# A third buffer for the key rows, and weights and x loaded ahead of the last four transfers of zeros, in a four-layer graph network

## The reference, cut to what matters

```
gathered = edge_weight[:, None] * x[edge_col]
neigh = segment_sum(gathered, edge_row, 3125)
out = x @ w_self + neigh @ w_neigh + bias        # weight = [w_self; w_neigh], 512 x 256
x = layernorm(x + out)
```

## Time and profile before

| | |
|---|---|
| Median of 3 runs | 3868.58 us (3865.46, 3868.58, 15440.14) |
| Profiled execution | 3860.42 us, span 3858.6 us |
| Instructions | 61183 |
| Busy in the span | PE 81%, PEld 47%, DVE 59%, ACT 37%, POOL 44% |
| DMA | 621.76 MB, mean 161 GB/s |
| Mean granted clock of TensorE | 0.891 of full speed |

### The profile page before, as it was taken

The page is one execution under the profiler, slowest core; times in us unless marked ns, Lnnn a source line. Parts: engine busy times, 40 slices in busy tenths (PEclk is TensorE's granted clock), DMA queues, the critical chain, the costliest instruction groups (busy, mean ns, idle before and its releaser), DMA issues. The chain is left out here.

```text
span 3858.6 us, 61183 instructions
## 1 busy us (share of the span) xinstructions
PE 3120.0 (81%) x16127; PEld 1811.6 (47%) x16128; DVE 2281.6 (59%) x5544; ACT 1443.9 (37%) x3080; POOL 1694.2 (44%) x1703
## 2 busy tenths in 40 slices
PE   4547999988997787777779957769864799998996
PEld 2114444666775343376634435644333444544543
DVE  7556333567898987655799965689867401202104
ACT  0000222478897565431056634036644402302202
POOL 3777772055002777616777752767772000000000
PEclk6678999999999898878989978779976899999998
DMA  9997889388654345366711105944452231231221
GB/s 400 404 365 258 311 295 302 100 248 247 174 148 115 101 138 153 105 241 194 211 25 27 27 18 189 309 139 138 128 178 84 84 97 44 82 97 53 92 89 34
DMA packets 381401, 621.76 MB, mean 161 GB/s; under 512 B 129149, under 2 KB 259926, under 8 KB 374098
## 3 DMA queue, kind: packets, MB, share of 16 engines
q1 hardware_dynamic: 229881, 353.10, 28.8%
q0 software_dynamic: 68112, 130.86, 11.9%
q10 hardware_dynamic: 83213, 135.59, 9.5%
HBM read 453.68 MB, written 169.22 MB: 161 GB/s over the span
## 5 line engine op out<-in xcount | busy, mean ns | idle before, releaser
L1464 ACT ACTIVATE onehot<-iota,drel 128x128 f32<-128x128 f32 x1248 | 381.5, 388 | 715.8 <-PE ps L1167 374.4
L1167 PE MATMUL ps<-shared_sb,onehot 128*128 128x264 f32 (+1 forms) x1600 | 558.8, 448 | 105.4 <-DVE accum L2252 100.5
L1227 PE MATMUL ps<-score_sb,shared_sb 128*128 128x512 f16 (+1 forms) x3150 | 624.9, 359 | 12.0 <-DVE shared_sb L2284 12.0
L2252 DVE TENSOR_TENSOR accum<-accum,ps 128x264 f32 (+1 forms) x1248 | 526.0, 421 | 12.1 <-issue 4.7
L740 POOL DMA_INDIRECT t_w<-early_sb x391 | 411.8, 1053 | 163.8 <-issue 89.6
L1227 PEld LDWEIGHTS ps<-score_sb,shared_sb 128*128 128x128 bf16 x3150 | 297.6, 98 | 335.0 <-issue 11.7
L1167 PEld LDWEIGHTS ps<-shared_sb,onehot 128*128 128x128 f32 x1600 | 266.2, 202 | 397.7 <-issue 233.4
L757 POOL TENSOR_SCALAR onehot<-iota,carry_d 98x512 bf16<-98x512 f32 x28 | 43.5, 1561 | 902.2 <-PE ps L1244 801.4
L776 POOL DMA_INDIRECT score_sb<-table,src_x x192 | 200.2, 1043 | 325.9 <-issue 300.8
L776 POOL DMA_INDIRECT shared_sb<-table,src_x x312 | 299.2, 959 | 100.4 <-issue 89.5
L2238 DVE TENSOR_TENSOR shared_sb<-shared_sb,ps 128x256 f32<-128x256 f32 x512 | 211.5, 413 | 67.9 <-DMA shared_sb<-table,src_x 50.4
(11 more groups left out here) (425 smaller groups left out, 5484.0 us busy)
## 6 DMA issues: line engine op xcount, KB each, us to landing
t_w<-onehot ACTq DMA_DIRECT2D x13, 6400.0 KB
score_sb<-t_adj SPq DMA_DIRECT2D x90, 640.0 KB, 3.9
accum<-t_hot SPq DMA_DIRECT2D x208, 256.0 KB
t_hot<-shared_sb SPq DMA_DIRECT2D x104, 256.0 KB
resid_sb<-t_w SPq DMA_DIRECT2D x13, 1664.0 KB
resid_sb<-t_w SPq DMA_DIRECT2D x13, 1536.0 KB
score_sb<-t_w SPq DMA_DIRECT2D x12, 1664.0 KB
shared_sb<-t_adj SPq DMA_DIRECT2D x30, 640.0 KB, 9.2
```

The lines of the kernel that those rows point to most:

```text
L1167: pe.matmul(ps[:, RING[(HU * h + u) % len(RING)], 0:w], onehot[:, h % 2 * HU + u, :], around[g][place(g, i, h)][:, u, 0:w], start=True, st ...
L1227: mm = pe.matmul(ps[:, 2 * (i % 3) + f, 0:w], h_gin[:, t, m, f * P:(f + 1) * P], ring["gin"][:, at % HOLD, c, 0:w], start=(t == 0 and m == ...
L1464: last = act.activation(onehot[:, h % 2 * HU + u, :], iota[:, 0:P], ACT.Abs, bias=drel[:, bass.ds(step + u, 1)], scale=-1.0)
L2252: dve.tensor_tensor(to, to, bank.unsqueeze(1), ALU.add).then_inc(step_acc, 1)
```

## The change

There are three buffers of key rows in place of two (`KEYS` = 3); the third takes the unused space of `key_gap`. Load i waits for the comparisons of load i-3. Its third semaphore is `adj_in[4]`, whose later use counts on from there. The third load waits besides for `values`, since the space is used for the weights' parts before. ACT's code for comparisons and the waits on `key_used` and `same_act` go. The block of ACT's other transfers becomes a function, `late_loads`, that is called in the loop of zeros at n = 9: nine transfers of zeros have then been issued and eight have landed; four are issued after it. None of the transfers changes its size or form.

```
+KEYS = 3
+LATE = 9
-        wide_key = [... for buf in (shared_sb[:, 2176:...], resid_sb[:, 5120:...])]
-        key_gap = flat_a[:, 4224:4224 + 2 * L0H * P].rearrange("p (u e) -> p u e", u=2)
+        wide_key = [... for buf in (shared_sb[:, 2176:...], resid_sb[:, 5120:...],
+                                    flat_a[:, 4224:4224 + 2 * L0H * P])]
...
             def two_quads(i):
-                if i >= 2:
-                    sp.wait_ge(*count("same_dve", 2 * i - 2))
-                    sp.wait_ge(*count("key_used", 2 * i - 2))
-                sp.dma_start(wide_key[i % 2]..., on_each(t_key, i * 2 * L0H, 2 * L0H)).then_inc(key_in[i % 2], 16)
+                if i == KEYS - 1:
+                    sp.wait_ge(*count("values", 1))
+                if i >= KEYS:
+                    sp.wait_ge(*count("same_dve", 2 * i - 2 * KEYS + 2))
+                sp.dma_start(wide_key[i % KEYS]..., on_each(t_key, i * 2 * L0H, 2 * L0H)).then_inc(key_in[i % KEYS], 16)
...
+            def late_loads():
+                act.wait_ge(*count("attr_split", 1))
+                act.wait_ge(*count("adj_ev", 1))
+                act.dma_start(t_attr...)      # attr_out
+                act.dma_start(rows[:, :, :], a["rows"])      # ld_rows
+                act.dma_start(vecs[:, :, :], a["vecs"])      # ld_vecs
+                act.dma_start(weights[:, :, 0:D], a["L0_gnn_weight"]...)      # ld_w0
+                act.dma_start(cols[:, :, :], a["x_cols"]...)      # ld_x
+                act.dma_start(hrows[:, :, 0:D], a["x_pad"]...)      # ld_xh
             for n in range(PIECES + 2):
                 if n >= 2:
                     act.wait_ge(attr_in[n % 2], 16 * (n // 2))
                     act.sem_inc(done("w_zero"), 1)
+                if n == LATE:
+                    late_loads()
                 if n < PIECES:
                     act.dma_start(parts_w[(n - 1) % PIECES], no_sums).then_inc(attr_in[n % 2], 16)
-            (the same two waits and six transfers, here, behind the loop)
...
             def compare(k):      # DVE
-                dve.wait_ge(key_in[k // 2 % 2], 16 * (k // 4) + 16)
+                dve.wait_ge(key_in[k // 2 % KEYS], 16 * (k // 2 // KEYS) + 16)
```

More of the change, by code:

```diff
@@ L47 @@
 QUADS = ET // L0H
-FIRST = QUADS
+KEYS = 3
 BATCHES = [2, 2, 4] + [8] * 11 + [2]
@@ L238, in build @@
         lo_rows_i = flat_k[0:SQ, 5472:5984].rearrange("p (b e) -> p b e", b=SB).bitcast(I32)
-        wide_key = [buf.rearrange("p (h e) -> p h e", h=2) for buf in (shared_sb[:, 2176:2176 + 2 * L0H * P], resid_sb[:, 5120:5120 + 2 * L0H * P])]
-        key_gap = flat_a[:, 4224:4224 + 2 * L0H * P].rearrange("p (u e) -> p u e", u=2)
+        wide_key = [buf.rearrange("p (h e) -> p h e", h=2) for buf in (shared_sb[:, 2176:2176 + 2 * L0H * P], resid_sb[:, 5120:5120 + 2 * L0H * P],
+                                                                      flat_a[:, 4224:4224 + 2 * L0H * P])]
         ring = {"gcn": shared_sb[:, 0:HOLD * GRP * CW // 2].bitcast(F16).rearrange("p (r c w) -> p r c w", r=HOLD, c=GRP),
@@ L298, in build @@
         key_in = [sem(f"key_in{h}") for h in range(2)]
-        in_four, so_far = attr_in + key_in, [16 * len(range(h, PIECES, 2)) for h in range(2)] + [16 * len(range(n, QUADS // 2, 2)) for n in range(2)]
+        in_four, so_far = attr_in + key_in, [16 * len(range(h, PIECES, 2)) for h in range(2)] + [16 * len(range(n, QUADS // 2, KEYS)) for n in range(2)]
         adj_in = [sem(f"adj_in{r}") for r in range(HOLD)]
         adj_kept = adj_in[0:len(STAGED)]
-        kept_before = [16 * PAIRS] * len(STAGED) + [0] * (HOLD - len(STAGED))
+        key_in = key_in + [adj_in[len(STAGED)]]
+        kept_before = [16 * PAIRS] * len(STAGED) + [16 * len(range(2, QUADS // 2, KEYS))] + [0] * (HOLD - len(STAGED) - 1)
         adj_used = sem("adj_used")
@@ L329, in build @@
                   [(f"{n}{k}", c) for k in (1, 2) for n, c in (("gat_in", NC), ("self_sub", 1), ("gat_out", NG))] + [("elu2", NC)],
-                  [("weighted1", 2), ("self_w1", 1), ("weighted2", 2), ("self_w2", 1)], [("diag_clear", 1), ("apart", S // QU), ("gaps", 3 * (S // HU))], [("x1_back", 16), ("x2_back", 16)], [("quad_sum", QUADS), ("own_mm", NT), ("adj_turned", BLOCKS * PAIRS)], [("same_act", QUADS), ("adj_staged", BLOCKS * PAIRS)], [("w_summed", QUADS), ("own_sum", NT)], [("step_mask", EB), ("te", 1), ("adj_rows", 1), ("adj_ev", 1), ("keys", 2), ("pre", 1), ("attr_split", 1)], [("te_ps", 3), ("adj_tp", 1), ("steps_ps", 2), ("steps_ev", 1), ("early_one", 1)],
+                  [("weighted1", 2), ("self_w1", 1), ("weighted2", 2), ("self_w2", 1)], [("diag_clear", 1), ("apart", S // QU), ("gaps", 3 * (S // HU))], [("x1_back", 16), ("x2_back", 16)], [("quad_sum", QUADS), ("own_mm", NT), ("adj_turned", BLOCKS * PAIRS)], [("adj_staged", BLOCKS * PAIRS)], [("w_summed", QUADS), ("own_sum", NT)], [("step_mask", EB), ("te", 1), ("adj_rows", 1), ("adj_ev", 1), ("keys", 2), ("pre", 1), ("attr_split", 1)], [("te_ps", 3), ("adj_tp", 1), ("steps_ps", 2), ("steps_ev", 1), ("early_one", 1)],
                   [("p0_" + n, c) for n, c in parts], [("rest_" + n, c) for n, c in parts],
@@ L938, in marks @@
                 pe.wait_ge(*count("same_dve", k + 1))
-                pe.wait_ge(*count("same_act", k + 1))
                 if kk == 0:
@@ L1366, in _ @@
             parts_w = t_w.rearrange("(k p n w) o -> k p n (w o)", k=PIECES, p=P, w=W_ZERO // 2)
+            def late_loads():
+                act.wait_ge(*count("attr_split", 1))
+                act.wait_ge(*count("adj_ev", 1))
+                act.dma_start(t_attr.rearrange("(b q) e -> q b e", b=SB), attr_b.rearrange("p b m e -> p b (m e)")).then_inc(done("attr_out"), 16)
+                act.dma_start(rows[:, :, :], a["rows"]).then_inc(done("ld_rows"), 16)
+                act.dma_start(vecs[:, :, :], a["vecs"]).then_inc(done("ld_vecs"), 16)
+                act.dma_start(weights[:, :, 0:D], a["L0_gnn_weight"].rearrange("(c p) n -> p c n", p=P)).then_inc(done("ld_w0"), 16)
+                act.dma_start(cols[:, :, :], a["x_cols"].rearrange("(c p) n -> p c n", p=P)).then_inc(done("ld_x"), 16)
+                act.dma_start(hrows[:, :, 0:D], a["x_pad"].rearrange("(t p) d -> p t d", p=P)).then_inc(done("ld_xh"), 16)
             for n in range(PIECES + 2):
@@ L1952, in compare @@
                 h = k % 2
-                dve.wait_ge(key_in[k // 2 % 2], 16 * (k // 4) + 16)
+                dve.wait_ge(key_in[k // 2 % KEYS], 16 * (k // 2 // KEYS) + 16)
                 if k >= 2:
                     dve.wait_ge(*count("quad_sum", k - 1))
-                for u in range(L0H if k < FIRST else L0H - 1):
-                    last = dve.tensor_scalar(same_key[h][:, u, :], wide_key[k // 2 % 2][:, h, :], adj_f[:, k * L0H + u:k * L0H + u + 1], None, ALU.is_equal)
+                for u in range(L0H):
+                    last = dve.tensor_scalar(same_key[h][:, u, :], wide_key[k // 2 % KEYS][:, h, :], adj_f[:, k * L0H + u:k * L0H + u + 1], None, ALU.is_equal)
                 last.then_inc(done("same_dve"), 1)
```

5 lines of the change are left out of this document (1 added, 4 removed).

## The result

The changed kernel took 3845.11 us (median of five runs, 3839.48 to 3849.53), the one before 3868.58 us beside it (one of its five executions took 15440.14 us and stands outside the ratio): a ratio of 0.994 with a 95% interval of 0.9926 to 0.9955, so 23 us less, and a forecast of 20. The profiled execution took 3845.11 us with a span of 3843.2 us, against 3858.6 us before; between the two profiled spans lie 15.4 us. The profiled execution of the kernel before was 8 us faster than its median, that of the changed kernel was its median.

The account below looks back on a forecast made before the run. Key loads through two buffers pace the marks, then PE's pairs bound. PE's start 22 us earlier, less 2 us cold clock, gives 20 us off the 3868.6 us median: 3849 us, own range 3838 to 3862, eight in ten 3812 to 3871.

Parts of the forecast that it names:

- The third buffer: Marks: key load period 6.3 to 4.2 us, 17 to 21 of 91.3 us waiting stay, marks end 72 us earlier.
- One turn for one packet: SP's 27 small-row transfers before the pairs: each small packet waits for one large zeros packet; PE starts at 341 us.
- The first rival: SP's small rows pass zeros in bundles or unhindered; first pair at 309 us, gain 52, 3817 us; chance 0.2.
- The second rival: Key loads get no faster, DMA service being the wait; marks end at 330 to 337 us, 3866 us; chance 0.1.
- The third: Rival: mixed DMA work slows; zeros end at 342 us, PE starts at 371, 3876 us; chance 0.1.
- The cold clock: PE's start of the pairs: after idling it starts at 1.2 GHz, first 10 us at mean 0.79, costing 2 us.
- The moved loads: ACT's queue: late loads issued at about 175 us after eight zeros landed, x there at about 237 us.
- That wait is avoided: Own products at 266 us would have waited 45 us for x in the old order; moving the loads avoids it.
- POOL's scatter: POOL's zeros waits pass in time, so its scatter ends at 606 us as before.
- limit of 65 us: POOL's slack: last pair begins near 686 us and could at about 620, so no gain exceeds some 65 us.
- only shifts: Everything after the pairs was claimed to move in time without changing length.

Follow-up runs that it names:

- the last experiment: Changed kernel with weights and x back behind all transfers of zeros, three key buffers kept, in a set without pauses: 3848.11 us, ratio 0.9948 to the kernel before.
- The doubled comparisons: Changed kernel with every DVE comparison of keys done twice, once into unused space: 5359.15 us beside 5142.4, one execution of each.

## Why the prediction was right

The forecast was 3849 us, and 3845.11 came. The mechanism was right as far as PE's start of the pairs (22.6 us earlier for 22); that the total agrees so well is in part luck, since the two profiled executions differ by 15.4 us and the medians by 23.5, with 20 forecast. The steps, by its own parts:

- **The third buffer.** The waits for keys fell to 25.9 us (17 to 21 forecast), and the own products began at 272.73 us (266). About 65 us off the marks for 72: the step is right and a little too large, by the 5 to 9 us more that DVE still waited. The last key load is issued at 256.78 us for 252.
- **One turn for one packet.** The wait for the small rows is 17.4 us (17), SP's 27 transfers are issued over 39.23 us ("40 us or more", missed by 1), the zeros had landed at 316 us (314), PE's start is 340.67 us (341). The zeros in rows of half the size confirm the mechanism (17.4 to 7.1 us). Until the zeros' end 181 rows of the 27 transfers passed per engine where the sum has 148, since from 307 us on more small rows than zeros passed; the late start of the 27 (289.5 us for 283) was made good by that. The rule was right, but the earlier trace rows, on which the prediction rested it, could not show it: that store was issued at 407.19 us, none of its packets started before 410, and from 410 to 412 us 22 of its packets passed beside 59 large ones. The earlier trace rows was the better support. The first rival, with the first pair at 309 us, fell, but not by the counts alone: it let small rows go in bundles and large ones singly. By the Trainium skill's rule of whole packets of 9 to 17 descriptors in a turn (DMA: Bandwidth & Descriptors, Queues, rings and completion order) both queues would bundle, and 942 rows beside 953 would fit that too; against it stand the start times of the packets (small rows no more often 10 to 40 ns apart than by chance, but 200 to 210 ns). The second rival (keys no faster) fell as well: SP's loads were mostly 4.0 to 4.1 us apart around 100 us. The third needed zeros later than 336 us in this kernel; they ended at 316.
- **The cold clock.** PE's first 10 us in the pairs ran at 0.68 against 1.00 before the change (windows of 340 to 350 and 363 to 373 us): 10 x 0.32 = 3 us, forecast 2.
- **The moved loads.** They were issued from 174.62 us (175), and x by rows landed at 237 us (237). "That wait is avoided", 45 us: it measured 43.46 where they are not moved. But the prediction didn't say that avoiding it is worth next to nothing while SP's queue ends later than x: 2.8 us of start, by the last experiment. It had both chains in one sum and took the later one, so its total did not suffer.
- **POOL's scatter "ends at 606 us as before".** Wrong: its last transfer began at 619.71 us against the 605.41 of the earlier trace rows. From 100 to 200 us it did 63 transfers where the earlier trace rows has 71. POOL's timeline of the changed kernel shows a transfer without and some beside comparisons:

```profile
149.51 0.96 POOL L742 DMA_INDIRECT t_w<-early_sb  x1 [0.30 <-DMA t_w<-early_sb]
150.77 1.22 POOL L742 DMA_INDIRECT t_w<-early_sb  x1 [0.30 <-issue]
152.30 1.28 POOL L742 DMA_INDIRECT t_w<-early_sb  x1 [0.30 <-issue]
```

  DVE's comparisons began at 150.12 us. The doubled comparisons show the same cause made large, and so does the kernel with zeros in rows of half the size. It cost the pairs nothing: SP was still issuing their loads at 656.99 us, and its only waits in that stage were for PE. The "limit of 65 us" is therefore some 14 us smaller than told, and was not reached.
- **What lies behind.** The pairs take 355.1 us from first to last start, 349.9 before; 3 us of that is the cold clock, and PE's waits without a shown releaser grew from 7.3 to 9.7 us. The prediction had "only shifts" and 2 us. With 22.6 - 5.2 = 17.4 us the last pair is earlier by just what the trace says (695.8 against 713.2 us), and the span by 15.4. The further 6 to 8 us to the medians' 23 are in no stage that a trace shows; the spread between the runs is as large (10 us).

So where did the other 43 of the 65 us go? Into SP's queue. From its last key load to the first pair's load it took 352.91 - 327.62 = 25.3 us before and takes 330.00 - 256.78 = 73.2 us now, 48 more: 20.6 in the 27 transfers, 15.4 in the wait for the small rows (17.4 for 2.0), 12 in issuing those, all because they now lie before the zeros' end instead of behind it; the last key load itself comes 70.8 us earlier, and 70.8 - 47.9 = 23. Take the 27 transfers away and 22 of the next 34 us go to ACT, which waits for the zeros' end.

**Open.** What a version gains in which ACT's first copies do not stand behind the wait for the zeros (it was not tried); by how much the 27 transfers behind the pairs' loads beat the changed kernel (ratios of 0.9919 and 0.994 to the same kernel, with intervals that overlap, from two sets; the pairs' end 9.4 us earlier in the traces); whether the comparisons hold up POOL by a port or by something else that both use; and what makes the pauses of some 10 us (each set ran on another chip at another time, and chip and time can't be told apart).

## What to carry to other kernels

When a wait is removed ahead of a point where several queues meet, follow each queue to that point with the traffic that it will then lie in: a transfer that was cheap behind a bulk fill costs one of the fill's packets for each of its own rows once it lies beside it. Issue what the next stage waits for ahead of small rows that nobody needs yet, and look for the next in-order engine that counts the fill as done before it does the stage's work. A transfer moved out of a wait of 45 us is worth only the distance to the chain that ends next.

## What the hardware showed that was not expected

DVE's comparisons lengthen POOL's indirect transfers: in the timelines of 100 to 270 us a transfer that overlaps one takes 1.22 us in the median (97 transfers), one that doesn't 0.96 (7; 40 in the kernel before), and with DVE busy for 98.10 or 99.96 of 100 us POOL did 27 or 11 in place of 63, single ones taking 11.77 or 26.21 us. Two queues with work took turns row by row, whatever the rows' sizes, so halving the rows of the bulk fill let the key loads of the other queue come faster (last one 24.5 us earlier) at the price of a fill that ends 8 us later. And the same kernel that takes 3869 us took near 5100 us in five sets of runs, with pauses of some 10 us in work that passes between engines, while its transfers kept their rate (406 against 407 GB/s from 100 to 200 us in the changed kernel).
